# A mask moved from the first stage's products into the contraction's chunks, with two changes of order

## The chip, the cores and the metric

The kernel runs on one core of a Trainium2 chip. The core has five engines that work side by side: TensorE (PE, matmuls), VectorE (DVE), ScalarE (ACT), GpSimd (POOL) and SyncE (SP), which here only issues DMAs. They meet through semaphores. The metric is the device time of one execution in microseconds (us), as the median of several runs; less is better.

## The reference

The input x is 256 x 256 pixels of 64 channels, all in fp32. With m the mask (256 x 256), what is computed is:

```
a      = layernorm(channel_norm(x))                     # over the 64 channels
left   = m * (a @ WL + bL) * sigmoid(a @ GL + gL)
right  = m * (a @ WR + bR) * sigmoid(a @ GR + gR)
t[i,j,c] = sum_k left[i,k,c] * right[j,k,c]             # one 256x256x256 product for each channel
x1     = x + (layernorm(t) @ WO + bO) * sigmoid(a @ G + g)
out    = x1 + mixture(layernorm(x1))                    # 8 experts 64x64, the best 2 by a router
```

The change concerns the factor m of left and right.

## The kernel before

There are three stages, and each engine runs its own program, written out by hand, with waits on semaphores.

**First stage.** x comes in 8 super-blocks of 32 rows, a row being 128 partitions x 2 pixels (q = 0, 1) x 64 channels. For each super-block VectorE makes the statistics (`bn`, L860), GpSimd the scale and shift (`rstd_a`, L356 to L365) and the normalized rows (`norm_a`: a multiplication L380, an addition L384, eight rows each). TensorE turns four rows at a time (`turn`, L646) and multiplies each pair of rows by the four weights (`project`, L658) into `pr_a`, a ring of three pairs in PSUM: the first half holds left and right, the second the gates. ScalarE puts the sigmoid of the gates into `sig_a` (L510). VectorE then does in `left_right` (L873), for each row of a pair and each q, one product `pr_a * mask * sig_a` of 128 columns: four for a pair, 512 in all. The mask enters as a scalar for each partition, `mt[:, row, q]`. The products go into `stage` (two blocks of 16 rows) and from there to `left_right_scratch` in DRAM (`block_a`). VectorE's own order puts the statistics of super-block s + 2 between the products of super-block s, from the seventh pair on. The SP queue issues, in its order: loads of x (each waits until GpSimd has scaled the super-block that held the buffer), stores of blocks, and toward the end early loads of the first chunks.

**Contraction.** The 64 channels are done in 8 chunks of 8 channels. `chunk` has two buffers of four parts, left and right for q = 0 and 1, 2048 columns each. `load_blocks` fetches a chunk, the left parts when an earlier packing has freed them, the right parts when TensorE has finished the chunk before the last. All parts of a buffer count on one semaphore, `chunk_in[b]`. GpSimd's `pack_left` (L401) copies the left parts into another order (two instructions of 2048 columns a chunk; in chunk 0 the last two blocks, which come straight from `stage` by `direct`, have two small ones of their own) and waits for the whole chunk. The packing of a chunk may begin when TensorE is done with the chunk before the last. TensorE (`chunk_b`, L696) makes for each of the 8 channels k two halves of 256 rows in one of four banks of `ein`; ScalarE copies the even k to `t_all` (L533), VectorE the odd k (L922), in a loop over the chunks. TensorE waits for the copy of k before it writes k + 4.

**Last stage.** 64 units of 8 columns by 128 partitions, in slots: slot u handles the experts of unit u, the gate of unit u + 4 and the output of unit u - 1. Each engine goes through its list in `slot`. A unit has eight tiles m = 0 to 7. TensorE broadcasts the routing weight (`bcast`, L783), for tiles 0, 2, 4, 6 and, in even units, 7 VectorE multiplies it by the doubled input (`scale`, L1036); for tiles 1, 3, 5 and in odd units 7 ScalarE copies it out first (L579) and GpSimd multiplies (L451). `expert(ep)` (L796) takes the tiles 2 ep and 2 ep + 1. ScalarE's `double` (L563) copies the input of the next unit to both halves of the partitions, its `gate` (L553) makes the sigmoid for which TensorE's `x_turn` (L727) waits, and `y_turn` (L804) turns the result of the unit before.

Of the kernel before, what the change touches and what calls it, by code (L numbers as in the profile page):

```python
# [8 lines left out]
ALU = mybir.AluOpType  # L9
# [95 lines left out]
def metaformer_kernel(nc, x, mask, weights, router_w, router_b, expert_w, expert_b, out):  # L105
# [6 lines left out]
    with ExitStack() as ctx:  # L112
# [3 lines left out]
        def keep(name, shape, dt=F32):  # L116
            return ctx.enter_context(nc.sbuf_tensor(name, shape, dt))
# [29 lines left out]

        setup_bytes = 4 * (12 * C + 4 + 6 * C + 6 * C + P + E * C + E + 2 * P + 2 * N)
        (xts, _, w_proj, mt, r_all, b_all, xa, xs, sig_a, stage, bst, nv, nh, ny, nt) = layer([
            ("xts", [P, 2, TURN * P]), ("skip_setup", [P, setup_bytes // 4 - 2 * TURN * P + 16]),  # L150
            ("w_proj", [P, 6 * C]),
            ("mt", [P, N, Q]), ("r_all", [P, N, Q]), ("b_all", [P, N, Q]),
            ("xa", [P, 2, SUPER, Q * C]), ("xs", [P, 2, SUPER, Q * C]),
# [16 lines left out]
        def left_packed(c, b):  # L170
# [5 lines left out]

        (_, sel, kind, xc, xn, tn, ttn, xtn, sig_c, x2t, x2d, zb, bcs, wt, outc, bst_t, bst_x, y32, rr, bt, lg, ls, m1, m2, pm, ws, pk) = layer([
            ("t_keep", [P, C, 2 * N]),
            ("sel", [P, 2, E, C], F32R), ("kind", [P, 4, E]),
            ("xc", [P, XC, UNIT_J, C]), ("xn", [P, UNIT_J, C]), ("tn", [P, UNIT_J, C]),  # L180
            ("ttn", [P, WIDE]), ("xtn", [P, WIDE]), ("sig_c", [P, WIDE]), ("x2t", [P, X2, WIDE]), ("x2d", [P, 2, 2, WIDE]),
            ("zb", [P, NZ, WIDE]), ("bcs", [P, 2, WIDE]), ("wt", [P, 2, WIDE], F32R),
            ("outc", [P, 2, UNIT_J, C]), ("bst_t", [P, 2, TOK // 2, 6]), ("bst_x", [P, 2, TOK // 2, 6]),
            ("y32", [P, 2 * TOK]), ("rr", [P, 2, 2 * TOK]), ("bt", [P, 2, TOK]), ("lg", [P, 2, TOK, E]), ("ls", [P, TOK, E]),
            ("m1", [P, TOK]), ("m2", [P, TOK]), ("pm", [P, TOK]), ("ws", [P, 2, TOK]),
            ("pk", [P, TOK, 2, 2 * E], F32R)])

# [50 lines left out]
        def _(sp):  # L239
# [10 lines left out]
            def load_blocks(c, b, blocks, parts=range(2 * Q)):  # L250
                for u in parts:
                    part = lr_dram.rearrange("n p (u c) -> u p n c", u=2 * Q)[u, :, blocks, c * RUN:(c + 1) * RUN]
                    sp.dma_start(chunk[:, b, u, blocks, :], part).then_inc(chunk_in[b], 16)

# [71 lines left out]
        def _(pool):  # L326
# [69 lines left out]

            loads = 2 * Q * 16

            def pack_left(c, b, blocks):
                for q in range(Q):  # L400
                    ins = pool.tensor_copy(  # L401
                        left_packed(c, b)[:, q, :, :].rearrange("p c (n r) -> p n c r", r=ROWS)[:, blocks, :, :],
                        chunk[:, b, 2 * q, blocks, :].rearrange("p n (c r) -> p n c r", c=CHUNK))
                return ins

            pool.wait_ge(xs_ready, SUPERS * PIECES)
            pool.wait_ge(chunk_in[0], PARTS[0] * loads)
            pack_left(0, 0, slice(0, BLOCKS - 2))
            pool.wait_ge(direct_in, loads)
            pack_left(0, 0, slice(BLOCKS - 2, BLOCKS)).then_inc(packed, 1)  # L410
            for c in range(1, CHUNKS):
                pool.wait_ge(chunk_in[c % 2], (c // 2 + PARTS[c % 2]) * loads)
# [74 lines left out]
        def _(act):  # L487
# [6 lines left out]
            for h in range(2):  # L494
                for q in range(Q):
                    ins = act.activation(mt[:, h * P:h * P + P, q], ps_set[:, 1, (2 * h + q) * P:(2 * h + q + 1) * P], ACT.Copy)
            ins.then_inc(set_act, 1)
# [92 lines left out]
            def slot(u, ku):  # L590
                odd = ku % 2 == 1
                if has(u):
                    bcast(3, u, ku)
                if has(u + 4):
                    front(u + 4)
                if odd and has(u + 1):
                    soft((u - 1) // 2)
                if has(u):
                    bcast(5, u, ku)
                if has(u + 1):  # L600
                    double(u + 1, ku + 1, 0)
# [18 lines left out]
        def _(pe):  # L620
# [194 lines left out]
            def slot(u, ku):  # L815
# [36 lines left out]
        def _(dve):  # L852
# [11 lines left out]
            def left_right(p):  # L864
# [324 lines left out]
```

## Time and profile before

| what | value |
|---|---|
| median of 3 runs | 1099.11 us (1098.92 to 1100.91) |
| the profiled execution's own time | 1097.87 us |
| its span in the profile | 1096.1 us |
| busy: PE, DVE, ACT, POOL | 1005.4, 869.5, 639.3, 749.7 us |
| first stage, to VectorE's last product | 215.2 us |
| contraction, to TensorE's last matmul | 335.0 us |
| data moved by DMA | 119.38 MB |

The profile is of one execution; its span begins with the first instruction and ends with the last. The busy times are averages over stages with different limits, so a change is read in its own stage: which engine the others wait for there.

### The profile page before, as it was taken

The page shows a single profiled execution, that of the slowest core. Times are in us where ns is not written, and L with a number is a line of the kernel's source. Part 1 is how long each engine was busy: PE and PEld are TensorE (multiplying, and loading weights), DVE is VectorE, ACT ScalarE, POOL GpSimd, SP SyncE. Part 2 cuts the span into 40 slices and gives each one's busy share as a digit, 9 for nine tenths or more (in the row PEclk, how much of TensorE's full clock was granted, in tenths as well). Part 3 has the DMA queues.
Part 4 walks back from the last instruction along what each step waited for, and adds up shares of the span by engine and source line. Part 5 has one row for each costly group of instructions (what it writes and reads, how often), then busy time and mean ns, then how long its engine had stood idle before and what let it go on. Part 6 is the DMA issues. An engine that isn't in the chain of part 4 may idle for free.

```text
span 1096.1 us, 18926 instructions
## 1 busy us (share of the span) xinstructions
PE 1005.4 (92%) x5658; PEld 552.8 (50%) x5658; DVE 869.5 (79%) x3030; ACT 639.3 (58%) x1134; POOL 749.7 (68%) x727
## 2 busy tenths in 40 slices
PE   4889999899994599999999999999999999999996
PEld 2566666688883344444444444444444444444432
DVE  5899999812216678898889988998899889988884
ACT  2556666611111356767676767676767767676754
POOL 5998888212223367878787878787878877787844
PEclk9999999999996689999999999999999999999999
DMA  7688679989951001111111111111111111111001
GB/s 181 193 281 296 231 259 299 344 272 294 293 158 39 20 25 53 39 58 39 60 39 59 40 59 39 58 40 59 40 55 42 49 50 44 54 40 59 30 30 39
DMA packets 98904, 119.38 MB, mean 109 GB/s; under 512 B 6390, under 2 KB 72182, under 8 KB 96758
## 3 DMA queue, kind: packets, MB, share of 16 engines
q1 hardware_dynamic: 97670, 117.75, 33.7%
q8 instruction: 46, 0.75, 0.3%
q10 hardware_dynamic: 1136, 0.46, 0.2%
q14 instruction: 52, 0.43, 0.1%
HBM read 67.33 MB, written 50.33 MB: 107 GB/s over the span
## 4 chain that ended last, share of the span: by engine, by line
PE 60%; ACT 16%; DVE 12%; issue 4%; DMA 4%; POOL 3%; SPq 0%; DVEq 0%; ACTq 0%; POOLq 0%
PE b_m L796 15%; PE ein L696 8%; PE ring L783 7%; PE b_d L744 7%; ACT x2d L563 6%; DVE stage L873 6%; PE pr_a L658 4%; PE b_g L727 4%; PE b_g L721 3%; ACT ttn L546 3%; DVE bst L860 3%; PE b_g L734 3%; PE b_t L721 3%; DMA chunk<-left_right_scratch 2%; ACT sig_c L553 2%
## 5 line engine op out<-in xcount | busy, mean ns | idle before, releaser
L451 POOL TENSOR_TENSOR zb<-bcs,x2d 128x512 f32<-128x512 f32 x224 | 286.4, 1281 | 170.5 <-ACT bcs L579 170.4
L796 PE MATMUL b_m<-zb,w_exp 128*64 128x512 f32 x1024 | 275.5, 617 | 0.2
L1036 DVE TENSOR_TENSOR zb<-ring,x2d 128x512 f32<-128x512 f32 x288 | 197.7, 687 | 61.4 <-PE ring L783 57.0
L579 ACT ACTIVATE bcs<-ring 128x512 f32<-128x512 f32 x224 | 133.3, 595 | 160.0 <-PE ring L783 155.8
L563 ACT ACTIVATE x2d<-x2t 64x512 f32<-64x512 f32 x256 | 160.6, 628 | 3.4
L873 DVE SCALAR_TENSOR_TENSOR stage<-pr_a,mt,sig_a 128x128 f32<-128x128 f32 x512 | 147.8, 419 | 11.3 <-ACT sig_a L510 11.2
L658 PE MATMUL pr_a<-w_proj,xts 64*128 64x256 f32 x1024 | 138.3, 400 | 14.5 <-DVE stage L873 14.0
L783 PEld LDWEIGHTS ring<-wt,sel 64*128 64x128 f32 x512 | 47.9, 184 | 168.4 <-DVE zb L1036 81.2
L783 PE MATMUL ring<-wt,sel 64*128 64x512 f32 x512 | 127.6, 495 | 3.1 <-DVE zb L1036 2.3
L510 ACT ACTIVATE sig_a<-pr_a 128x512 f32<-128x512 f32 x128 | 76.5, 597 | 71.3 <-PE pr_a L658 71.2
L658 PEld LDWEIGHTS pr_a<-w_proj,xts 64*128 64x128 f32 x1024 | 95.3, 190 | 42.9 <-issue 23.6
L437 POOL TENSOR_TENSOR tn<-t_all,rr 128x512 f32<-128x512 f32 x64 | 86.8, 1357 | 35.5 <-DVE rr L964 21.0
L922 DVE COPY t_all<-ein 128x512 f32 x32 | 22.1, 691 | 93.2 <-PE ein L696 93.2
L744 PE MATMUL b_d<-turn_route,x2t 128*128 128x144 f32 x512 | 84.0, 310 | 3.3 <-DVE x2t L1053 3.3
L696 PE MATMUL ein<-chunk,t_all 128*128 128x256 f32 x384 | 83.6, 380 | 1.2 <-POOL t_all L401 1.2
L796 PEld LDWEIGHTS b_m<-zb,w_exp 128*64 128x64 f32 x1024 | 51.0, 134 | 62.4 <-issue 60.2
L744 PEld LDWEIGHTS b_d<-turn_route,x2t 128*128 128x128 f32 x512 | 69.7, 198 | 19.4 <-issue 14.6
L696 PEld LDWEIGHTS ein<-chunk,t_all 128*128 128x128 f32 x384 | 72.8, 190 | 11.8 <-issue 1.9
L734 PE MATMUL b_g<-xtn,w_og 64*64 64x512 f32 x256 | 71.1, 629 | 7.6 <-ACT ttn L546 7.6
L546 ACT ACTIVATE ttn<-b_t 64x512 f32<-64x512 f32 x128 | 75.8, 592 | 1.5
L533 ACT ACTIVATE t_all<-ein 128x512 f32 x32 | 19.1, 597 | 96.9 <-PE ein L696 96.9
L1059 DVE BATCH_NORM_STATS2 bst_x<-b_d 128x6 f32<-128x128 f32 x256 | 67.2, 285 | 5.9 <-PE b_d L744 5.9
(131 smaller groups left out, 1784.7 us busy)
## 6 DMA issues: line engine op xcount, KB each, us to landing
left_right_scratch<-stage SPq DMA_DIRECT2D x16, 2048.0 KB, 7.9
chunk<-left_right_scratch SPq DMA_DIRECT2D x24, 1024.0 KB, 9.1
xc<-in_x SPq DMA_DIRECT2D x64, 256.0 KB, 2.8
out<-outc SPq DMA_DIRECT2D x64, 256.0 KB, 2.0
chunk<-left_right_scratch SPq DMA_DIRECT2D x12, 384.0 KB, 7.8
chunk<-left_right_scratch SPq DMA_DIRECT2D x8, 192.0 KB, 5.1
chunk<-left_right_scratch SPq DMA_DIRECT2D x4, 256.0 KB, 8.0
chunk<-left_right_scratch SPq DMA_DIRECT2D x8, 64.0 KB, 4.8
```

Source lines behind the costliest of these rows:

```text
L451: pool.tensor_tensor(zb[:, m % NZ, :], bcs[:, tiles_before(POOL_TILES, ku, ku, m) % 2, :], x2d[:, ku % 2, m % 2, :], ALU.mult)\
L546: ins = act.activation(ttn[half * C:(half + 1) * C, :], b_t[(1 - half) * C:(2 - half) * C, :], ACT.Copy)
L563: ins = act.activation(x2d[half * C:(half + 1) * C, kw % 2, t, :], x2t[t * C:(t + 1) * C, kw % X2, :], ACT.Copy)
L579: act.activation(bcs[:, tiles_before(POOL_TILES, ku, ku, m) % 2, :], ring[:, bcast_bank(ku % 2, m), :], ACT.Copy).then_inc(bcast_out, 1)
L658: ins = pe.matmul(pr_a[:, k, q, r * LRG:(r + 1) * LRG], xts[half, g % 2, col:col + P], w_proj[half, 0:LRG], start=True, stop=True)
L696: m = pe.matmul(ein[:, k % 4, h * N:h * N + N], left_packed(c, b)[:, q, k, h * P:h * P + P], right[:, q, :, k, :], start=q == 0, stop=q == 1)
L734: g = pe.matmul(b_g[half[t], :], w_og[half[t], 0, :], xtn[half[t], :], start=True, stop=True)
L744: m = pe.matmul(b_d[:, j // 2, j % 2 * BACK:(j % 2 + 1) * BACK], x2t[:, kw % X2, pairs[j]], turn_route[:, :], start=True, stop=True)
L783: pe.matmul(ring[:, bcast_bank(ku % 2, m), :], sel[rows, ku % 2, m // 2 * 2:m // 2 * 2 + 2, :].rearrange("p e c -> p (e c)"), wt[rows, ku ...
L796: ins = pe.matmul(b_m[t * C:(t + 1) * C, :], w_exp[:, ep, :], zb[:, (2 * ep + t) % NZ, :], start=False, stop=ep == EP - 1, skip_group_chec ...
L873: ins = dve.scalar_tensor_tensor(stage[:, n % 2, q, :, row], pr_a[:, p % PAIR_RING, q, r * LRG:r * LRG + 2 * C], mt[:, n * ROWS + row:n * ...
L1036: dve.tensor_tensor(zb[:, m % NZ, :], ring[:, bcast_bank(ku % 2, m), :], x2d[:, ku % 2, m % 2, :], ALU.mult)\
```

## The change

It has three parts.

1. *Mask.* `left_right` is now one product of `pr_a` and `sig_a` of 512 columns for a pair, without the mask. GpSimd's packing multiplies the left part by the mask instead of copying it. VectorE multiplies the right parts by the mask in place (`mask_right`, two instructions of 2048 columns a chunk, four in chunk 0), and TensorE waits for it on the new semaphore `masked`. The mask of chunks 0 and 1 is done before VectorE's loop over the chunks, that of chunk c + 1 after the copy k = 5 of chunk c. `mt` lies in another order, and `ttn` takes its memory over later. VectorE's loop over the chunks is written out.
2. *Counts.* The parts of a chunk count on two semaphores: left parts on `left_in[b]`, for which GpSimd waits, right ones on `chunk_in[b]`, for which VectorE and TensorE wait.
3. *Order in the last stage.* ScalarE does `gate(u + 4)` before the second `double`, TensorE does `expert(2)` before `y_turn`.

```
 def load_blocks(c, b, blocks, parts=range(2 * Q)):
-    sp.dma_start(chunk[:, b, u, blocks, :], part).then_inc(chunk_in[b], 16)
+    sp.dma_start(chunk[:, b, u, blocks, :], part).then_inc(chunk_in[b] if u % 2 else left_in[b], 16)
...
+def mask_of(q, blocks):
+    return mt[:, q, :].rearrange("p (n r) -> p n r", r=ROWS)[:, blocks, :].unsqueeze(2)\
+        .broadcast_to([P, blocks.stop - blocks.start, CHUNK, ROWS])
...
 def pack_left(c, b, blocks):                      # GpSimd
-    ins = pool.tensor_copy(
+    ins = pool.tensor_tensor(
         left_packed(c, b)[:, q, :, :].rearrange("p c (n r) -> p n c r", r=ROWS)[:, blocks, :, :],
-        chunk[:, b, 2 * q, blocks, :].rearrange("p n (c r) -> p n c r", c=CHUNK))
+        chunk[:, b, 2 * q, blocks, :].rearrange("p n (c r) -> p n c r", c=CHUNK), mask_of(q, blocks), ALU.mult)
-pool.wait_ge(chunk_in[0], PARTS[0] * loads)
+pool.wait_ge(left_in[0], PARTS[0] * loads)
...
 # ScalarE's slot
+    if has(u + 4):
+        gate(u + 4)
     if has(u + 1):
         double(u + 1, ku + 1, 1)
-    if has(u + 4):
-        gate(u + 4)
...
 # TensorE
     pe.wait_ge(packed, c + 1)
+    pe.wait_ge(masked, c + 1)
...
     if has(u + 4):
         out_gate(u + 4)
+    if has(u):
+        expert(2, u, ku)
     if has(u - 1):
         y_turn(u - 1, ku - 1)
-    if has(u):
-        expert(2, u, ku)
...
 # VectorE, left_right
-    for r in range(PAIR):
-        row = p * PAIR % ROWS + r
-        for q in range(Q):
-            ins = dve.scalar_tensor_tensor(
-                stage[:, n % 2, q, :, row], pr_a[:, p % PAIR_RING, q, r * LRG:r * LRG + 2 * C],
-                mt[:, n * ROWS + row:n * ROWS + row + 1, q], sig_a[:, p % PAIR_RING, q, r, :], ALU.mult, ALU.mult)
-    ins.then_inc(lr_done, 1)
+    row, k = p * PAIR % ROWS, p % PAIR_RING
+    dve.tensor_tensor(stage[:, n % 2, :, :, row:row + PAIR].rearrange("p q c r -> p q r c"),
+                      pr_a[:, k, :, :].rearrange("p q (r c) -> p q r c", r=PAIR)[:, :, :, 0:2 * C],
+                      sig_a[:, k, :, :, :], ALU.mult).then_inc(lr_done, 1)
...
-with dve.Fori(0, CHUNKS) as c:
+def mask_right(b, blocks):
+    for q in range(Q):
+        right = chunk[:, b, 2 * q + 1, blocks, :].rearrange("p n (c r) -> p n c r", c=CHUNK)
+        ins = dve.tensor_tensor(right, right, mask_of(q, blocks), ALU.mult)
+    return ins
+
+def chunk_landed(c):
+    dve.wait_ge(chunk_in[c % 2], (c // 2 + PARTS[c % 2]) * Q * 16)
+
+chunk_landed(0)
+mask_right(0, slice(0, BLOCKS - 2))
+dve.wait_ge(direct_in, 2 * Q * 16)
+mask_right(0, slice(BLOCKS - 2, BLOCKS)).then_inc(masked, 1)
+chunk_landed(1)
+mask_right(1, slice(0, BLOCKS)).then_inc(masked, 1)
+for c in range(CHUNKS):
     for k in range(1, CHUNK, 2):
         dve.wait_ge(ein_ready, c * CHUNK + k + 1)
-        dve.tensor_copy(t_all[:, bass.ds(c * CHUNK + k, 1), :].rearrange("p a n -> p (a n)"), ein[:, k % 4, :])\
-           .then_inc(ein_dve, 1)
+        dve.tensor_copy(t_all[:, c * CHUNK + k, :], ein[:, k % 4, :]).then_inc(ein_dve, 1)
+        if k == 5 and 0 < c < CHUNKS - 1:
+            chunk_landed(c + 1)
+            mask_right((c + 1) % 2, slice(0, BLOCKS)).then_inc(masked, 1)
```

## Rows read from the trace of the kernel before

**Rows 1.** Window: length; busy PE, PEld, DVE, ACT, POOL; clock, DMA share, GB/s.
```profile
120.00:160.00 40.00, 35.82 (x268) 25.04 (x266) 38.59 (x158) 23.71 (x40) 31.64 (x46) 1.00 0.76 264
```

**Rows 2.** Timeline of GpSimd in the first stage: start, us, engine, line, tiles, idle.
```profile
80.19 0.27 POOL L356 TENSOR_SCALAR nv<-bst 128x64 f32<-128x64 f32 x1
...
86.47 3.76 POOL L380 TENSOR_TENSOR xs<-xa,r_all 128x1024 f32<-128x1024 f32 x2
...
90.19 3.76 POOL L384 TENSOR_TENSOR xs<-xs,b_all 128x1024 f32<-128x1024 f32 x2
...
104.05 0.27 POOL L356 TENSOR_SCALAR nv<-bst 128x64 f32<-128x64 f32 x1 [2.66 <-DVE bst L860]
...
176.04 0.28 POOL L356 TENSOR_SCALAR nv<-bst 128x64 f32<-128x64 f32 x1 [2.77 <-DVE bst L860]
```

**Rows 3.** Timeline of all engines, the first stage's last turns and products.
```profile
205.93 0.65 PE L646 MATMUL xt_a<-turn_route,xs 128*128 128x128 f32 x4
...
208.44 0.66 PE L646 MATMUL xt_a<-turn_route,xs 128*128 128x128 f32 x4
...
210.84 4.37 DVE L873 SCALAR_TENSOR_TENSOR stage<-pr_a,mt,sig_a 128x128 f32<-128x128 f32 x16 [0.26 <-ACT sig_a L510]
```

**Rows 4.** Costliest groups of the page: busy us, mean ns, idle before.
```profile
L451 POOL TENSOR_TENSOR zb<-bcs,x2d 128x512 f32<-128x512 f32 x224 | 286.4, 1281 | 170.5 <-ACT bcs L579 170.4
...
L1036 DVE TENSOR_TENSOR zb<-ring,x2d 128x512 f32<-128x512 f32 x288 | 197.7, 687 | 61.4 <-PE ring L783 57.0
...
L873 DVE SCALAR_TENSOR_TENSOR stage<-pr_a,mt,sig_a 128x128 f32<-128x128 f32 x512 | 147.8, 419 | 11.3 <-ACT sig_a L510 11.2
```

**Rows 5.** Timeline of all engines, from the first stage into the contraction.
```profile
216.52 4.24 POOL L401 COPY xa<-chunk 128x1792 f32<-128x1792 f32 x4 [19.27 <-DMA chunk<-left_right_scratch]
...
220.00 0.50 DVE L916 TENSOR_TENSOR bias_lo<-eb_wide,bias_hi 128x256 fp32r<-128x256 f32 x1
...
220.90 15.74 PE L696 MATMUL ein<-chunk,xa 128*128 128x256 f32 x64 [3.18 <-POOL xa L401]
...
229.43 3.73 POOL L401 COPY t_all<-chunk 128x2048 f32<-128x2048 f32 x2 [8.68 <-DMA chunk<-left_right_scratch]
...
236.47 13.98 PE L696 MATMUL ein<-chunk,t_all 128*128 128x256 f32 x64
```

**Rows 6.** The chain that ended last, the load of chunk 2's right half.
```profile
237.07 10.05 DMA chunk<-left_right_scratch
```

**Rows 7.** Timeline of all engines in chunk 2: its start, the copy k = 5.
```profile
251.04 4.15 PE L696 MATMUL ein<-chunk,t_all 128*128 128x256 f32 x18 [0.59 <-POOL t_all L401]
...
261.82 0.69 DVE L922 COPY t_all<-ein 128x512 f32 x1 [2.76 <-PE ein L696]
```

**Rows 8.** Timeline: VectorE and GpSimd products from SBUF at one time.
```profile
346.55 0.69 DVE L1071 TENSOR_TENSOR xn<-xc,rx 128x512 f32<-128x512 f32 x1 [1.67 <-PE b_t L721]
...
346.61 1.81 POOL L437 TENSOR_TENSOR tn<-t_all,rr 128x512 f32<-128x512 f32 x1 [2.40 <-PE b_t L721]
...
347.27 1.70 DVE L1073 TENSOR_TENSOR xn<-xn,bx 128x512 f32<-128x512 f32 x1
```

**Rows 9.** One microsecond of chunk 0, columns as in rows 1.
```profile
222.00:223.00 1.00, 1.00 (x3) 0.75 (x3) 0.00 (x0) 0.00 (x0) 0.00 (x0) 0.50 1.24 524
```

**Rows 10.** Timeline of the last stage: GpSimd's tile 5, TensorE's y turn.
```profile
506.33 1.28 POOL L451 TENSOR_TENSOR zb<-bcs,x2d 128x512 f32<-128x512 f32 x1
...
507.36 0.66 PE L804 MATMUL ring<-turn_route,x2t 128*128 128x128 f32 x4
```

**Rows 11.** The chain that ended last, through an odd and an even unit.
```profile
599.70 1.18 PE b_d L744 x8
...
609.39 0.44 PE ring L811 x4
...
611.27 1.18 PE b_d L744 x8
...
621.87 1.18 PE b_d L744 x8
```

More of the change, by code:

```diff
@@ L130, in metaformer_kernel @@
         bx = keep("bx", [P, 2 * N])
+        mt = keep("mt", [P, Q, N])
         def layer(tensors, psums=()):
@@ L148, in metaformer_kernel @@
         setup_bytes = 4 * (12 * C + 4 + 6 * C + 6 * C + P + E * C + E + 2 * P + 2 * N)
-        (xts, _, w_proj, mt, r_all, b_all, xa, xs, sig_a, stage, bst, nv, nh, ny, nt) = layer([
+        (xts, _, w_proj, r_all, b_all, xa, xs, sig_a, stage, bst, nv, nh, ny, nt) = layer([
             ("xts", [P, 2, TURN * P]), ("skip_setup", [P, setup_bytes // 4 - 2 * TURN * P + 16]),
             ("w_proj", [P, 6 * C]),
-            ("mt", [P, N, Q]), ("r_all", [P, N, Q]), ("b_all", [P, N, Q]),
+            ("r_all", [P, N, Q]), ("b_all", [P, N, Q]),
             ("xa", [P, 2, SUPER, Q * C]), ("xs", [P, 2, SUPER, Q * C]),
@@ L174, in left_packed @@
             return left_odd if b else left_even
-        (_, sel, kind, xc, xn, tn, ttn, xtn, sig_c, x2t, x2d, zb, bcs, wt, outc, bst_t, bst_x, y32, rr, bt, lg, ls, m1, m2, pm, ws, pk) = layer([
+        def mask_of(q, blocks):
+            return mt[:, q, :].rearrange("p (n r) -> p n r", r=ROWS)[:, blocks, :].unsqueeze(2)\
+                .broadcast_to([P, blocks.stop - blocks.start, CHUNK, ROWS])
+        (_, sel, kind, xc, xn, tn, xtn, sig_c, x2t, x2d, zb, bcs, wt, outc, bst_t, bst_x, y32, rr, bt, lg, ls, m1, m2, pm, ws, pk) = layer([
             ("t_keep", [P, C, 2 * N]),
@@ L180, in metaformer_kernel @@
             ("xc", [P, XC, UNIT_J, C]), ("xn", [P, UNIT_J, C]), ("tn", [P, UNIT_J, C]),
-            ("ttn", [P, WIDE]), ("xtn", [P, WIDE]), ("sig_c", [P, WIDE]), ("x2t", [P, X2, WIDE]), ("x2d", [P, 2, 2, WIDE]),
+            ("xtn", [P, WIDE]), ("sig_c", [P, WIDE]), ("x2t", [P, X2, WIDE]), ("x2d", [P, 2, 2, WIDE]),
             ("zb", [P, NZ, WIDE]), ("bcs", [P, 2, WIDE]), ("wt", [P, 2, WIDE], F32R),
@@ L186, in metaformer_kernel @@
             ("pk", [P, TOK, 2, 2 * E], F32R)])
+        ttn = mt[:, :, :].rearrange("p q n -> p (q n)")
         (b_t, b_g, b_d, b_r, b_m, ring) = layer([], [
@@ L211, in metaformer_kernel @@
         turn_ready = sem("turn_ready"); turned = sem("turned")
-        chunk_in = [sem("chunk_in0"), sem("chunk_in1")]
-        direct_in = sem("direct_in"); packed = sem("packed"); ein_ready = sem("ein_ready"); ein_act = sem("ein_act"); ein_dve = sem("ein_dve")
+        chunk_in = [sem("right_in0"), sem("right_in1")]; left_in = [sem("left_in0"), sem("left_in1")]
+        direct_in = sem("direct_in"); packed = sem("packed"); masked = sem("masked"); ein_ready = sem("ein_ready"); ein_act = sem("ein_act"); ein_dve = sem("ein_dve")
         xc_in = [sem("xc_in0"), sem("xc_in1"), sem("xc_in2")]; sel_made = sem("sel_made")
@@ L395, in _ @@
                 norm_a(s, (2, 3))
-            loads = 2 * Q * 16
+            loads = Q * 16
             def pack_left(c, b, blocks):
                 for q in range(Q):
-                    ins = pool.tensor_copy(
+                    ins = pool.tensor_tensor(
                         left_packed(c, b)[:, q, :, :].rearrange("p c (n r) -> p n c r", r=ROWS)[:, blocks, :, :],
-                        chunk[:, b, 2 * q, blocks, :].rearrange("p n (c r) -> p n c r", c=CHUNK))
+                        chunk[:, b, 2 * q, blocks, :].rearrange("p n (c r) -> p n c r", c=CHUNK), mask_of(q, blocks), ALU.mult)
                 return ins
             pool.wait_ge(xs_ready, SUPERS * PIECES)
-            pool.wait_ge(chunk_in[0], PARTS[0] * loads)
+            pool.wait_ge(left_in[0], PARTS[0] * loads)
             pack_left(0, 0, slice(0, BLOCKS - 2))
-            pool.wait_ge(direct_in, loads)
+            pool.wait_ge(direct_in, 2 * loads)
             pack_left(0, 0, slice(BLOCKS - 2, BLOCKS)).then_inc(packed, 1)
             for c in range(1, CHUNKS):
-                pool.wait_ge(chunk_in[c % 2], (c // 2 + PARTS[c % 2]) * loads)
+                pool.wait_ge(left_in[c % 2], (c // 2 + PARTS[c % 2]) * loads)
                 if c > 1:
@@ L495, in _ @@
                 for q in range(Q):
-                    ins = act.activation(mt[:, h * P:h * P + P, q], ps_set[:, 1, (2 * h + q) * P:(2 * h + q + 1) * P], ACT.Copy)
+                    ins = act.activation(mt[:, q, h * P:h * P + P], ps_set[:, 1, (2 * h + q) * P:(2 * h + q + 1) * P], ACT.Copy)
             ins.then_inc(set_act, 1)
@@ L683, in chunk_b @@
             def chunk_b(c, b):
-                loads = 2 * Q * 16
+                loads = Q * 16
                 first = PARTS[b] * loads
@@ L687, in chunk_b @@
                 if isinstance(c, int) and c == 0:
-                    pe.wait_ge(direct_in, loads)
+                    pe.wait_ge(direct_in, 2 * loads)
                 pe.wait_ge(packed, c + 1)
+                pe.wait_ge(masked, c + 1)
                 right = chunk[:, b, :, :, :].rearrange("p (q s) n (c r) -> p q s n c r", s=2, c=CHUNK)[:, :, 1, :, :, :]
```

## The prediction

> **What bounds the kernel now.** I read the windows first, then the chain that ended last, then the timelines of the places where the chain changes its engine.
>
> The first stage (to 215.2 us) is VectorE's. In 120 to 160 us it is busy 38.6 of 40 us, TensorE 35.8, GpSimd 31.6 [rows 1]. GpSimd starts a new super-block (32 rows) 24 us after the last one, and waits 2.66 us of that for VectorE's statistics: 104.05 in [rows 2] carries the wait, 80.19 none. Its own work is therefore 104.05 - 2.66 - 80.19 = 21.2 us a super-block. TensorE needs 2.51 us for each four rows when nobody holds it [rows 3], 20.1 us for 32. So VectorE (24.0) is first, GpSimd (21.2) and TensorE (20.1) close behind.
>
> The contraction (eight chunks) is TensorE's: a chunk takes 13.98 us, and the next begins 14.57 us after it began where a transfer and a packing lie between [rows 5, 7]. It is tight: right halves land 10.05 us after they are asked for [rows 6]. Here VectorE and GpSimd have much idle time, but both are in TensorE's loop.
>
> The last stage is 32 pairs of units. The even unit takes 621.87 - 611.27 = 10.60 us, the odd one 11.57 [rows 11]. TensorE's work in the odd one is only one turn of 0.44 us more, so it stalls 11.57 - 10.60 - 0.44 = 0.53 us, behind ScalarE, whose sigmoid comes after four copies.
>
> **First stage: what goes.** 512 three-operand products of 128 columns become 128 products of 512. The busy time gives 147.8/512 = 0.289 us each, 1.15 us a pair; the nearest row for the new one (PSUM times SBUF, 512 columns, same engine) is 0.687 [rows 4]. It saves 0.46 us a pair, 7.4 a super-block: VectorE falls from 24.0 to about 17 us. The output's stride is the old one and was paid in the old products, so I add nothing. The bound is not 17 but GpSimd's 21.2. From 80.19 four more of its super-blocks in a row put the start of the last at 80.19 + 4 x 21.2 = 165.0 instead of 176.04. The first eight rows are ready 90.19 - 80.19 + 1.9 = 11.9 us later [rows 2], at 176.9; seven more turns of 2.51 give 194.5; and from the last turn to VectorE's last product 215.21 - 208.44 = 6.8 us [rows 3], less some 0.5 since the last four products no longer queue, give 200.8. Gain: 215.2 - 200.8 = **-14.4 us**, not the 6 x 7 that VectorE alone would give. The SP queue holds block stores behind the loads of x, which wait for GpSimd's scaling; that comes at GpSimd's pace as well, so I allow 0 to 2 us of loss for it.
>
> **Contraction: where the mask goes.** GpSimd's packing turns from a copy into a product with two inputs. For the product of 2048 the bounds are 2 x 1.88 = 3.8 us (1024 columns with one broadcast input, 3.76 for two) and 4 x 1.281 = 5.1 (512 columns, both inputs full) [rows 2, 4]. The mask's inner run is full, so I take 4.5, that is 9.0 for a chunk. It starts when the chunk before begins, since the left half is now counted alone, and ends by +9 to +10 of a 14 us chunk: hidden, unless it is late. VectorE gets two products of 2048 columns. From 0.69 us for 512 [rows 8], one column a cycle, they are 2.3 each (0.69 x 4 = 2.8 above): **4.6 us a chunk, on the path**.
>
> *Chunks 2 to 7.* The mask of the next chunk stands in VectorE's queue behind the copy k = 5. After a wait that copy begins 261.82 - 251.04 = 10.78 us into the chunk and ends at 11.47 [rows 7]; the right half has landed by 10.1 [rows 6]. The mask runs from 11.5 to 16.1, and TensorE begins 0.1 later. So each chunk takes 16.2 us instead of 14.0 (twice 14.57), with the copy k = 7 queued behind the mask too, which delays nobody else. Six such steps: 6 x 16.2 - (2 x 14.57 + 4 x 13.98) = 97.2 - 85.1 = **+12.1 us**. The earlier packing saves only the two waits of 0.6 that this sum already drops.
>
> *Chunks 0 and 1.* Count from VectorE's last product (215.2). Before, TensorE began chunk 0 at +5.7 and chunk 1 at +21.3. GpSimd's packing of chunk 0 starts at +1.3 and would take 2 x 4.0 + 2 x 0.7 us (1792 and 256 columns at the same price) instead of the 4.24 of the copies; VectorE is free at +5.3 [rows 5]. Then the two meet. In [rows 8] VectorE's product runs 0.69 us undisturbed, and 1.70 when it starts while GpSimd's product of 1.81 us is under way: it ended 0.55 us after GpSimd's did, as if it had waited for the end and then run. The mask products have two SBUF inputs like that one. I let them run one after the other: packing to +9.3, then masks and the small last pieces alternately, masked at about +15, TensorE starts chunk 0 there. Chunk 1's data are there at +14.2 (229.43 [rows 5]), and VectorE waits for them and masks them before it copies the first odd column of chunk 0. With the packing of chunk 1 between, that lasts to +26; TensorE has done five of eight columns and waits. Three columns later, at +26.0 + 0.7 + 5.3 = +32, chunk 1 begins: **+10.7 us**. Bounds: +30 (GpSimd at 3.8, VectorE first) and +41 (next part).
>
> *The clock.* The idle 3.18 us before 220.90 were followed by a granted clock of 0.50, the 1.2 GHz level [rows 5, 9], and chunk 0 took 15.74 instead of 13.98: 1.8 us. The new gaps are 2.0 us each, for which I have no row. 0 to 6 x 1.8 = 10.8; I take **+3**.
>
> **Last stage.** ScalarE's sigmoid before the second pair of copies comes 1.27 us earlier, and would take away the 0.53 us of each odd unit: 32 x 0.53 = 17 us. But TensorE now does expert(2) before the y turn, and expert(2) needs GpSimd's tile 5, which ends at 506.33 + 1.28 = 507.61 where TensorE is free at 507.36 [rows 10]: 0.25 us of wait in every unit, even and odd alike. The odd one then ends 0.29 earlier, the even one 0.25 later. I take **0**, and 0.1 us of error in either reading is 6 us.
>
> **Sum.** 1096.1 - 14.4 + 12.1 + 10.7 + 3 + 0 = 1107.5 us of span. The profiled execution took 1.8 us more than its span (1097.87), and the median of the runs is 1.2 above it: 1107.5 + 3.0 = **1110.5 us**, +1.0%.
>
> **Rivals.**
> 1. *Strict turns at the start.* If after every instruction the other engine goes first, the two small masks of chunk 0 (the last two blocks) each wait for one 4.5 us packing of chunk 1. Chunk 0 is masked at +25 instead of +15, VectorE then masks chunk 1 at once, nothing stalls again, and chunk 1 begins at 25 + 14 + 1.8 = +41: 9 us more, about 1120. For it: one pair of rows with the waiting. Against: it needs chunk 1's left half to have landed before +15, which is close. 
> 2. *The last stage gains (the other side).* Should TensorE not wait for tile 5 (POOL spans are rough), 17 us go: 1094, faster. It decides from 11.4 + 2.2 = 13.6 of the 17 us on, that is, if the wait is under 0.05 us a unit. For it: expert(2) never waits for GpSimd now. Against: it stands 0.6 us later now.
> 3. *The clock falls in every chunk*: +7.8 on the sum, 1118.
> 4. *The masks cost nothing*, since right halves land earlier than k = 5 allows and VectorE overlaps: 1110.5 - 12.1 = 1098. The order of its queue speaks against it.
>
> **From cases to numbers.** My forecast 0.5 (own range 1104 to 1117), strict turns 0.2, clock 0.1, last-stage gain 0.12, masks free 0.03, the rest 0.05. The bounds of the prices add 5 either way; the range that leaves out 2 in 10 is 1097 to 1122. A measurement of this kernel tells about 0.2% (2.2 us) from no change. Faster 0.13 (rival 2, part of 4), same 0.05, slower 0.82.
>
> **What would show each step.** Right: products of 0.69 us in the first stage, GpSimd without waits for statistics after 80 us, last product near 201; a mask after each k = 5 and chunk starts 16.2 us apart; TensorE waiting for VectorE's mask before chunks 2 to 7 and for a copy in chunk 0; expert(2) waiting for GpSimd's tile 5. Wrong: chunk starts at 14 us, a first stage that ends later than 205, or units whose sum is off 22.17 us by over 0.2.

## The result, and the profile after

The changed kernel takes 1120.86 us (median of 4 runs, 1120.26 to 1123.33); before took 1099.01 on the same chip (4 runs, 1097.98 to 1100.91). The ratio is 1.020 (95% interval 1.0183 to 1.0217): slower by 2.0% (between 1.8 and 2.2), where 1.0% was predicted (1110.5). The profiled execution took 1120.89 us with a span of 1119.1, 23.0 more than before's 1096.1.

Two groups of part 5 of the page of the profile after (columns as in [rows 4]):

```profile
L806 PE MATMUL b_m<-zb,w_exp 128*64 128x512 f32 x1024 | 276.2, 616 | 21.0 <-POOL zb L460 19.4
...
L881 DVE TENSOR_TENSOR stage<-pr_a,sig_a 128x512 f32<-128x512 f32 x128 | 127.1, 1034 | 22.0 <-ACT sig_a L519 20.4
```

L881 is the new product of the first stage: 1034 ns each, not 687. L806 is `expert`: it sat idle for 21.0 us, 19.4 of them for GpSimd's tile. I read the rest in the order of the prediction's sum.

**First stage.** The timeline of VectorE before the change, the products of two pairs (four instructions each), with three statistics between them:

```profile
136.84 1.20 DVE L873 SCALAR_TENSOR_TENSOR stage<-pr_a,mt,sig_a 128x128 f32<-128x128 f32 x4
...
138.47 1.19 DVE L873 SCALAR_TENSOR_TENSOR stage<-pr_a,mt,sig_a 128x128 f32<-128x128 f32 x4
```

And after it, a pair's product among the statistics, and the last product:

```profile
134.58 1.03 DVE L881 TENSOR_TENSOR stage<-pr_a,sig_a 128x512 f32<-128x512 f32 x1
...
136.03 1.03 DVE L881 TENSOR_TENSOR stage<-pr_a,sig_a 128x512 f32<-128x512 f32 x1
...
204.93 1.01 DVE L881 TENSOR_TENSOR stage<-pr_a,sig_a 128x512 f32<-128x512 f32 x1 [0.22 <-ACT sig_a L519]
```

And of GpSimd, the first instruction of two super-blocks:

```profile
145.28 0.27 POOL L365 TENSOR_SCALAR nv<-bst 128x64 f32<-128x64 f32 x1 [0.86 <-DVE bst L870]
...
167.34 0.27 POOL L365 TENSOR_SCALAR nv<-bst 128x64 f32<-128x64 f32 x1 [0.88 <-DVE bst L870]
```

VectorE starts a product, and with three statistics behind it the next product, every 136.03 - 134.58 = 1.45 us; before the same turn took 138.47 - 136.84 = 1.63. GpSimd's period is 22.06 us (145.28 to 167.34), 0.88 of it a wait for the statistics; before it was 24.0 with 2.7 [rows 2]. The last product ends at 204.93 + 1.01 = 205.94 instead of 215.21: **-9.3 us**. This term carries about 1 us of scatter: in the six profiles with the old first stage (`before` and five kernels below) the last product ends between 215.16 and 217.20, in the six with the new one (`after` and five below) between 205.71 and 206.77.

**From the first stage to chunk 1.** Timelines of single stretches around the masks of chunk 0 (a row shows only the instructions that its window touches):

```profile
207.28 11.28 POOL L410 TENSOR_TENSOR xa<-chunk,mt 128x1792 f32<-128x1792 f32 x4 [18.74 <-DMA chunk<-left_right_scratch]
...
211.45 4.06 DVE L923 TENSOR_TENSOR bias_lo<-eb_wide,bias_hi 128x256 fp32r<-128x256 f32 x1
...
215.44 2.54 DVE L929 TENSOR_TENSOR chunk<-chunk,mt 128x1792 f32<-128x1792 f32 x1
...
216.06 2.50 POOL L410 TENSOR_TENSOR xa<-chunk,mt 128x256 f32<-128x256 f32 x1
...
217.90 2.54 DVE L929 TENSOR_TENSOR chunk<-chunk,mt 128x1792 f32<-128x1792 f32 x1
...
219.81 4.98 POOL L410 TENSOR_TENSOR t_all<-chunk,mt 128x2048 f32<-128x2048 f32 x1 [1.25 <-DMA chunk<-left_right_scratch]
...
220.36 4.71 DVE L929 TENSOR_TENSOR chunk<-chunk,mt 128x256 f32<-128x256 f32 x1
...
224.75 4.67 POOL L410 TENSOR_TENSOR t_all<-chunk,mt 128x2048 f32<-128x2048 f32 x1
...
225.00 4.71 DVE L929 TENSOR_TENSOR chunk<-chunk,mt 128x256 f32<-128x256 f32 x1
...
229.85 16.05 PE L706 MATMUL ein<-chunk,xa 128*128 128x256 f32 x64 [19.89 <-DVE chunk L929]
```

GpSimd's two long packings (1792 columns) run from 207.28 to 215.2. `bias_lo` (L923, an instruction with two SBUF inputs that took 0.50 us in [rows 5]) starts at 211.45 and ends at 215.51, 0.3 us after them. From there the engines alternate, one instruction each: behind the first small packing (256 columns) VectorE's mask of 1792 columns, the second small packing, the second mask of 1792. Then comes GpSimd's packing of chunk 1, 4.98 us, and VectorE's mask of 256 columns, started 0.55 us after it, needs 4.71; the second mask of 256 columns needs 4.71 as well, behind the second packing. In the chain that ended last the four masks of chunk 0 are one piece:

```profile
215.51 14.21 DVE chunk L929 x4
```

TensorE starts chunk 0 at 229.85, that is +23.9 from the last product (before: +5.7). Chunk 1 starts at 245.74, +39.8 instead of +21.3: **+18.5 us**.

**Chunks 1 to 7.** The chain that ended last, from chunk 1 into chunk 2:

```profile
256.30 0.69 DVE t_all L944
...
256.99 4.41 DVE chunk L929 x2
```

The timeline of TensorE, the contraction's chunks (L706 is `chunk_b`):

```profile
245.74 13.98 PE L706 MATMUL ein<-chunk,t_all 128*128 128x256 f32 x64
...
261.63 14.08 PE L706 MATMUL ein<-chunk,t_all 128*128 128x256 f32 x64 [1.92 <-DVE chunk L929]
...
277.65 15.76 PE L706 MATMUL ein<-chunk,t_all 128*128 128x256 f32 x64 [1.94 <-DVE chunk L929]
...
346.68 3.69 PE L706 MATMUL ein<-chunk 128*128 128x256 f32 x16 [1.93 <-DVE chunk L929]
```

Each of the chunks 2 to 7 waits 1.9 us for the mask, which stands behind the copy k = 5 (L944), as drawn. But in some chunks the same 64 matmuls take 15.76 instead of 14.08. Three windows, columns as in [rows 1]:

```profile
262.00:264.00 2.00, 2.00 (x11) 1.77 (x10) 0.00 (x0) 0.24 (x1) 1.78 (x1) 1.00 1.02 292
...
278.00:280.00 2.00, 2.00 (x7) 1.62 (x6) 0.00 (x0) 0.00 (x0) 2.00 (x1) 0.57 1.09 309
...
282.00:284.00 2.00, 2.00 (x11) 1.74 (x11) 0.69 (x1) 0.00 (x0) 2.00 (x1) 1.00 1.15 345
```

The granted clock is 1.00 (2.4 GHz) at the start of the chunk that began at 261.63, and 0.57 (nearly the 1.2 GHz level) at the start of the one at 277.65, where it is back at 1.00 from 282 us on. Both chunks followed an idle gap of 1.92 to 1.94 us. Chunk 1 to chunk 7 takes 346.68 - 245.74 = 100.94 us where before took 84.57: **+16.4**.

**Last stage.** The chain that ended last, through one odd and one even unit (as [rows 11]):

```profile
602.25 1.18 PE b_d L754 x8
...
608.12 1.29 POOL zb L460
...
609.54 1.08 PE b_m L806 x4
...
613.52 1.18 PE b_d L754 x8
...
624.36 1.18 PE b_d L754 x8
```

The timeline of TensorE at the first of these waits:

```profile
609.54 1.08 PE L806 MATMUL b_m<-zb,w_exp 128*64 128x512 f32 x4 [0.31 <-POOL zb L460]
```

The odd unit takes 11.27 us, the even one 10.84; before 11.57 and 10.60 [rows 11]. From the start of chunk 7 to the end of the span it is 772.42 us instead of 775.06: **-2.6**. Together -9.3 + 18.5 + 16.4 - 2.6 = +23.0.

### The profile page after: what moved, and what is told of

The parts are those of the page before. It is cut to its first block, busy times and chain, and to the rows that moved or that the text cites. A ratio compares the mean times of both kernels' runs of the same rounds, so it can differ in the third digit from the quotient of the medians.

```text
span 1119.1 us, 18486 instructions
## 1 busy us (share of the span) xinstructions
PE 1004.0 (90%) x5658; PEld 559.2 (50%) x5658; DVE 895.9 (80%) x2664; ACT 644.4 (58%) x1134; POOL 799.0 (71%) x727
## 4 chain that ended last, share of the span: by engine, by line
PE 48%; POOL 21%; DVE 14%; issue 11%; ACT 4%; DMA 2%; DVEq 0%; POOLq 0%; SPq 0%
PE b_m L806 13%; PE ein L706 9%; POOL zb L460 9%; PE b_d L754 7%; POOL tn L446 6%; PE ring L793 5%; DVE stage L881 4%; PE pr_a L667 4%; DVE chunk L929 4%; PE ring L814 3%; ACT bcs L588 3%; POOL xn L445 3%; DVE bst L870 3%; PE b_g L737 2%; DMA left_right_scratch<-stage 2%
## 5 line engine op out<-in xcount | busy, mean ns | idle before, releaser
L806 PE MATMUL b_m<-zb,w_exp 128*64 128x512 f32 x1024 | 276.2, 616 | 21.0 <-POOL zb L460 19.4
L881 DVE TENSOR_TENSOR stage<-pr_a,sig_a 128x512 f32<-128x512 f32 x128 | 127.1, 1034 | 22.0 <-ACT sig_a L519 20.4
L806 PEld LDWEIGHTS b_m<-zb,w_exp 128*64 128x64 f32 x1024 | 52.5, 135 | 123.0 <-DVE zb L1060 69.2
L706 PE MATMUL ein<-chunk,t_all 128*128 128x256 f32 x384 | 89.4, 396 | 9.6 <-DVE chunk L929 9.6
L410 POOL TENSOR_TENSOR t_all<-chunk,mt 128x2048 f32<-128x2048 f32 x12 | 59.0, 4938 | 42.4 <-PE ein L706 34.1
L706 PEld LDWEIGHTS ein<-chunk,t_all 128*128 128x128 f32 x384 | 76.1, 199 | 22.8 <-issue 11.6
L944 DVE COPY t_all<-ein 128x512 f32<-128x512 f32 x32 | 22.1, 690 | 79.4 <-PE ein L706 79.4
L555 ACT ACTIVATE mt<-b_t 64x512 f32<-64x512 f32 x128 | 75.7, 591 | 1.5
```

Of the source, the lines that this page charges most:

```text
L706: m = pe.matmul(ein[:, k % 4, h * N:h * N + N], left_packed(c, b)[:, q, k, h * P:h * P + P], right[:, q, :, k, :], start=q == 0, stop=q == 1)
L806: ins = pe.matmul(b_m[t * C:(t + 1) * C, :], w_exp[:, ep, :], zb[:, (2 * ep + t) % NZ, :], start=False, stop=ep == EP - 1, skip_group_chec ...
L881: dve.tensor_tensor(stage[:, n % 2, :, :, row:row + PAIR].rearrange("p q c r -> p q r c"), pr_a[:, k, :, :].rearrange("p q (r c) -> p q r ...
```

## The experiments

The kernels are named by what they do; numbers are medians, with the ratio to before on the same chip and its interval.

### The two orders of the last stage, and the counts

Four kernels take one or two parts of the change into the kernel before. `gate_only`:

```
# ScalarE's slot, kernel before
+    if has(u + 4):
+        gate(u + 4)
     if has(u + 1):
         double(u + 1, ku + 1, 1)
-    if has(u + 4):
-        gate(u + 4)
```

> The kernel before with one edit: ScalarE's gate(u + 4) ahead of the second double. My theory: the 0.53 us stall of each odd unit goes and, since expert(2) stays behind the y turn, nothing waits for GpSimd's tile 5: pairs of units 22.17 - 0.53 = 21.64 us, 32 x 0.53 = 17 us less, about 1082. Rival: the second double is late for the next unit (it now waits behind the gate, which waits for TensorE's out_gate) and holds VectorE's and GpSimd's tiles: 1095 to 1100.

Measured: 1089.26 us, ratio 0.9906 (0.9886 to 0.9926), before 1099.59: 10.3 us faster. The odd unit takes 11.23 us, the even one still 10.60. The forecast was 1082: of the stall of 0.53 us only 11.57 - 11.23 = 0.34 went, and 0.19 stayed. Where it stayed shows in the timeline of VectorE and TensorE at the y turn of an odd unit:

```profile
604.07 0.68 DVE L1036 TENSOR_TENSOR zb<-ring,x2d 128x512 f32<-128x512 f32 x1
...
604.10 0.59 PE L734 MATMUL b_g<-xtn,w_og 64*64 64x512 f32 x1
...
604.80 0.42 PEld L804 LDWEIGHTS ring<-turn_route,x2t 128*128 128x128 f32 x4 [1.00 <-DVE zb L1036]
...
604.81 0.65 PE L804 MATMUL ring<-turn_route,x2t 128*128 128x128 f32 x4
```

The y turn (L804) starts when VectorE's tile is done, 0.71 us after the last matmul of the gate began (604.10 to 604.81); in the even unit that follows it starts 0.52 us after it (615.33 to 615.85). The difference is the 0.19. The 1.00 in brackets is idle time of the weight loads, while TensorE's matmuls still ran. The chain passes there through VectorE's routing arithmetic (L1008 to L1015), which stands before that tile in its queue. The gain of this order ended at the next engine in line, after 32 x 0.34 = 10.9 us by the units.

`expert_only` takes the other order:

```
# TensorE's slot, kernel before
+    if has(u):
+        expert(2, u, ku)
     if has(u - 1):
         y_turn(u - 1, ku - 1)
-    if has(u):
-        expert(2, u, ku)
```

> The kernel before with one edit: TensorE's expert(2) ahead of the y turn. My theory: expert(2) waits some 0.3 us for GpSimd's tile 5 in every unit; the even unit gets 0.25 us longer, the odd one stays at ScalarE's sigmoid: 32 x 0.25 = 8 us more, about 1107. Rival (the wait is hidden by TensorE's queue): 1099.

Measured: 1107.19 us, ratio 1.0063 (1.004 to 1.0085): 7.6 us slower. The turns b_d of successive units start at 560.78, 572.34 and 583.17, so the odd unit is as long as before (11.56) and the even one 10.84 instead of 10.60. 32 x 0.24 = 7.7 us: the wait for tile 5 that [rows 10] allowed to be read.

`both_orders` has the two edits:

> The kernel before with both changes of order and nothing else: the last stage of the changed kernel. Theory: its 22.11 us a pair of units, 1097. If the last stage gained more and the contraction lost more than I read from the traces: under 1094.

Measured over 10 runs: 1095.76 us, ratio 0.9969 (0.9957 to 0.9981): 3.8 us faster; the two alone add up to -2.7. Units of 10.84 and 11.27 us, as in the changed kernel.

`counts_only` takes the counts of left and right parts alone:

```
-    sp.dma_start(chunk[:, b, u, blocks, :], part).then_inc(chunk_in[b], 16)
+    sp.dma_start(chunk[:, b, u, blocks, :], part).then_inc(chunk_in[b] if u % 2 else left_in[b], 16)
...
-    pool.wait_ge(chunk_in[c % 2], ...)
+    pool.wait_ge(left_in[c % 2], ...)
```

> The kernel before with left and right halves counted apart, GpSimd still copying. Theory: the packing no longer waits for the right half, so the two waits of 0.6 us before chunks 2 and 4 go: chunks begin 14.0 us apart, 1098. Rival: the earlier packing lets the next left half be fetched earlier and delays right halves: 1099 to 1102.

Measured over 10 runs: 1097.33 us, ratio 0.9986 (0.9975 to 0.9998), 2.3 us faster. The timeline of TensorE, six chunks without a wait:

```profile
236.69 83.04 PE L696 MATMUL ein<-chunk,t_all 128*128 128x256 f32 x384
...
319.57 13.98 PE L696 MATMUL ein<-chunk 128*128 128x256 f32 x64
```

The two waits of 0.6 us [rows 7] are gone, and six steps take 82.9 us instead of 84.6. But the steps vary by themselves: `gate_only`, which has the old counts, takes 83.6 for them. So the counts give 0.7 to 1.7 us by the steps, and 2.3 by the medians.

### The product of the first stage

`wide_product` puts the new product of 512 columns into the kernel before. The mask is multiplied nowhere.

```
-    for r in range(PAIR):
-        ...
-            ins = dve.scalar_tensor_tensor(stage[:, n % 2, q, :, row], ..., ALU.mult, ALU.mult)
+    dve.tensor_tensor(stage[:, n % 2, :, :, row:row + PAIR].rearrange("p q c r -> p q r c"), ..., ALU.mult).then_inc(lr_done, 1)
```

> The kernel before with the one product of 512 columns a pair, and the mask multiplied in nowhere. It isolates the first stage. The changed kernel's trace shows 0.94 us a product instead of my 0.69, so VectorE stays first at 22.0 us a super-block: last product near 206, 9 us less, 1090, and chunk starts as before. If 0.69 had been right, GpSimd would bound it: 201, 1085.

`wide_plain` has the same product with its output written without gaps. The mask is multiplied nowhere here too, and left and right go to the scratch in another order than the contraction reads.

```
-    stage[:, n % 2, :, :, row:row + PAIR].rearrange("p q c r -> p q r c")
+    stage[:, n % 2].rearrange("p q c r -> p (q c r)")[:, row // PAIR * 512:row // PAIR * 512 + 512]
+        .rearrange("p (q r c) -> p q r c", q=Q, r=PAIR)
```

> As wide_product, but each product is written without gaps in stage instead of at every 16th element, so left and right lie in the wrong order in the scratch. Theory: the stride of the output costs the 0.25 us, a product takes 0.69 us, GpSimd becomes first (21.2 us a super-block), last product near 201, 1085. Rival: the order of the loops or PSUM costs it: 0.94 us again, 1090.

Measured: `wide_product` 1090.03 us, ratio 0.9915 (0.9893 to 0.9936); `wide_plain` 1084.67, ratio 0.9863 (0.984 to 0.9886); before 1099.50. In `wide_product` the product takes 1001 to 1076 ns and the last one ends at 206.7, GpSimd's period is 22.0 to 22.1 with 0.8 to 0.9 of waiting: the first stage of the changed kernel, without the rest of it. In `wide_plain` it takes 666 to 693 ns. Its timeline, VectorE's same turn of one product and three statistics, and the last product:

```profile
135.22 0.67 DVE L871 TENSOR_TENSOR stage<-pr_a,sig_a 128x512 f32<-128x512 f32 x1
...
136.40 0.68 DVE L871 TENSOR_TENSOR stage<-pr_a,sig_a 128x512 f32<-128x512 f32 x1
...
199.62 0.69 DVE L871 TENSOR_TENSOR stage<-pr_a,sig_a 128x512 f32<-128x512 f32 x1 [0.22 <-ACT sig_a L510]
```

And GpSimd's super-blocks in the same kernel:

```profile
122.50 0.28 POOL L356 TENSOR_SCALAR nv<-bst 128x64 f32<-128x64 f32 x1
...
143.77 0.27 POOL L356 TENSOR_SCALAR nv<-bst 128x64 f32<-128x64 f32 x1
```

1.18 us a turn, and GpSimd waits no more: 21.27 us a super-block, last product at 200.3. The prediction had 21.2 and 200.8 from 0.687 us. So the mechanism and the pace of GpSimd were right, and what was wrong is the product's price: its output goes to every 16th element of `stage` (64 bytes apart).

### The start of the contraction

`left_copy` is the changed kernel with GpSimd's packing a copy again. Left gets no mask.

```
-    ins = pool.tensor_tensor(left_packed(c, b)..., chunk[:, b, 2 * q, blocks, :]..., mask_of(q, blocks), ALU.mult)
+    ins = pool.tensor_copy(left_packed(c, b)..., chunk[:, b, 2 * q, blocks, :]...)
```

> The changed kernel with GpSimd copying the left halves again (they get no mask). Theory: the two engines still shut each other out at the start, but GpSimd's turns are 1.7 to 1.9 us instead of 4.0 to 4.6: masks of chunk 0 done at about +15 instead of +24 after the last product, chunk 1 begins at about +31 instead of +40; chunks 2 to 7 still 16.0 apart or 17.7 where the clock falls, since they wait for VectorE alone: about 1112. Rival (GpSimd's length matters for chunks 2 to 7 too): those come under 15 us apart and 1100.

One run: 1108.85 us, span 1107.1. Chunk 0 starts at +10.2 from the last product, chunk 1 at +28.0; +15 and +31 were expected, and 1112. VectorE is done with `bias_lo` at 211.3 here, since no long packing holds it, and masks chunk 0 in 5.02 us. Here the stall appears that the prediction drew for the changed kernel: TensorE does 40 of 64 matmuls, five columns, and waits for VectorE, which stands in the masks of chunk 1. The timeline of TensorE:

```profile
216.36 11.43 PE L706 MATMUL ein<-chunk,xa 128*128 128x256 f32 x40 [7.09 <-DVE chunk L929]
...
228.87 5.45 PE L706 MATMUL ein<-chunk,xa 128*128 128x256 f32 x24 [1.07 <-DVE t_all L944]
```

So GpSimd's arithmetic costs 39.8 - 28.0 = 11.8 us at the start and, with 12.0 us between the two spans, next to nothing later. That does not say whether its length or its place hurts.

`pack1_held` leaves the lengths and changes the place: in the changed kernel the packing of chunk 1 waits until chunk 0 is masked.

```
 for c in range(1, CHUNKS):
+    if c == 1:
+        pool.wait_ge(masked, 1)
     pool.wait_ge(left_in[c % 2], ...)
```

> The changed kernel with one wait more: GpSimd packs chunk 1 only when chunk 0 is masked. Theory (strict turns): the two small masks no longer wait behind packings of 4.6 us; chunk 0 begins at +16 instead of +24, masks of chunk 1 take turns with its packing until +30, TensorE stops after five columns and chunk 1 begins at about +33 to +35 instead of +40: 1114 to 1116. Rival (chunk 1's packing then is the last): no gain, 1121.

Measured: 1113.55 us, ratio 1.0132 (1.0108 to 1.0155), 7.3 us less than the changed kernel. The chain that ended last has the four masks of chunk 0 in

```profile
216.86 5.61 DVE chunk L931 x4
```

5.61 us instead of 14.21, and chunk 0 starts at +15.8, chunk 1 at +31.2. The prediction's own numbers for this place were +15 and +32. The first is met by its mechanism: the two small masks no longer stand behind long packings. The second is met partly by chance: VectorE masks chunk 1 until 231.2, +24.4, and the stall of TensorE that the prediction drew in chunk 0 does not come. Chunk 0 goes through without a wait, 15.4 us from start to start.

### The mask's place, and the clock

`mask_k3` is the changed kernel with the mask of the next chunk behind the copy k = 3.

```
-    if k == 5 and 0 < c < CHUNKS - 1:
+    if k == 3 and 0 < c < CHUNKS - 1:
```

> The changed kernel with the mask of the next chunk behind the copy k = 3 instead of k = 5. Theory: the place in VectorE's queue costs 1.3 us a chunk; now the mask starts when the right half lands (8.6 to 10.1 us into the chunk), ends at 13.2 to 14.6, chunks begin 14.2 to 14.7 us apart instead of 16.0, the gaps are under 1 us and the clock no longer falls: 6 x 1.3 + 3 x 1.7 = 13 us less, 1108. Rival (the copy k = 5 held behind the mask stops TensorE): chunks 16 us apart as now, 1121.

Measured: 1108.12 us, ratio 1.0081 (1.0056 to 1.0107), before 1098.27. The timelines of TensorE, then of GpSimd and VectorE at two of the masks:

```profile
261.77 14.08 PE L706 MATMUL ein<-chunk,t_all 128*128 128x256 f32 x64 [1.38 <-DVE chunk L929]
...
276.68 14.08 PE L706 MATMUL ein<-chunk,t_all 128*128 128x256 f32 x64 [0.84 <-DVE chunk L929]
...
291.37 14.08 PE L706 MATMUL ein<-chunk,t_all 128*128 128x256 f32 x64 [0.61 <-DVE chunk L929]
...
263.02 9.07 POOL L410 TENSOR_TENSOR t_all<-chunk,mt 128x2048 f32<-128x2048 f32 x2 [7.25 <-DMA chunk<-left_right_scratch]
...
269.59 6.86 DVE L929 TENSOR_TENSOR chunk<-chunk,mt 128x2048 f32<-128x2048 f32 x2
...
286.63 4.49 DVE L929 TENSOR_TENSOR chunk<-chunk,mt 128x2048 f32<-128x2048 f32 x2 [2.05 <-DMA chunk<-left_right_scratch]
```

The gaps shrink from 1.9 us to between 0.61 and 1.38, and after them no chunk is slow any more: each takes 13.9 to 14.1 us. They do not vanish. The right half lands late in the chunk, and a mask that meets a packing takes 6.86 us for two instructions instead of 4.49.

### The versions that could beat both

`gate_counts` is the kernel before with the gate's order and the counts, and nothing else of the change.

> The kernel before with the earlier gate and the separate counts, without the other order and with the mask where it was: the parts that gained alone. Theory: 10 + 2 us, 1087. Rival (they overlap): 1089.

Measured: 1087.44 us (1086.60 to 1088.38), ratio 0.990 (0.988 to 0.9919), before 1098.27. It is the fastest version that still computes everything.

`all_mended` is the changed kernel with the held packing of chunk 1, the mask behind k = 3, and `y_turn` before `expert(2)` again.

> The changed kernel with its mask moved as it is, but the y turn ahead of expert(2) again, the mask behind k = 3 and the packing of chunk 1 held until chunk 0 is masked. Theory, by addition from 1121: - 7 (held), - 13 (k = 3), - 6.5 (order): 1094. Moving the mask then still costs 7 us against gate_counts. Rival (held and k = 3 share their gain): 1098 or more.

Measured: 1090.60 us (1090.34 to 1091.06), ratio 0.9932 (0.9914 to 0.995), 3.4 us under what the addition gave. Faster than before, and 3.2 us slower than `gate_counts`, which leaves the mask where it was. TensorE's chunks:

```profile
221.21 15.80 PE L708 MATMUL ein<-chunk,xa 128*128 128x256 f32 x64 [12.57 <-DVE chunk L931]
...
236.84 13.98 PE L708 MATMUL ein<-chunk,t_all 128*128 128x256 f32 x64
...
266.57 27.89 PE L708 MATMUL ein<-chunk,t_all 128*128 128x256 f32 x128 [0.86 <-DVE chunk L931]
...
324.78 13.98 PE L708 MATMUL ein<-chunk 128*128 128x256 f32 x64
```

The last product ends at 205.7 here, 10.8 us before that of `gate_counts` (216.6); chunk 0 starts at 221.21 against 222.41. Nearly the whole gain of the first stage is spent there: packing and masks run one after the other (+15.5 from the last product instead of +5.8). The six steps then take 87.9 us against 82.9. Moving the mask costs 3 us even in its best version here. Not tried was a version whose product is written without gaps and whose contraction reads that order; `wide_plain` leaves out what such a version would have to pay for the reading.

## Why the prediction was right in direction and 10 us short

The forecast of a slower kernel came true; the size did not, 1110.5 against 1120.86. By span the forecast was 1107.5 and the result 1119.1, 11.6 more; the step from span to time was 1.8 us and not 3.0. By the terms of the sum:

| term | predicted | measured | off by |
|---|---|---|---|
| first stage, to the last product | -14.4 | -9.3 | +5.1 |
| from there to chunk 1 | +10.7 | +18.5 | +7.8 |
| chunk 1 to chunk 7, mask and clock | +12.1 + 3 | +16.4 | +1.3 |
| last stage | 0 | -2.6 | -2.6 |

**First stage: the right mechanism, a term mis-sized.** The step that failed is "The output's stride is the old one and was paid in the old products, so I add nothing". The nearest row had the same engine, the same columns and inputs from PSUM and SBUF, but wrote without gaps. So the old side of the difference, 1.15 us a pair, held whatever the stride costs, and the new side, 0.687, did not. `wide_plain` shows that with such an output the forecast is exact (200.3 for 200.8), and `wide_product` that with the kernel's own output the same instruction takes 1.03 us. By the turns of one product and three statistics, 1.63 us before, 1.45 after and 1.18 without gaps, the merged product saved 0.18 us a pair and not 0.46. Whether the old products paid the same per column is not shown: they also had more instructions to start. The Trainium skill (SBUF — State Buffer, "Door 1: The DMA port swizzle (why `[64,N]` ≈ `[32,N]`)") says that each access that crosses to a new 16-byte line pays a penalty. The difference of 1.03 and 0.69 us agrees in its direction; the Trainium skill gives no size there. With 1.45 us a turn VectorE has no wait from 131.10 to 145.1, and the statistics come late again, so the first stage did not become GpSimd's alone. The prediction had named this as a sign of being wrong: a first stage that ends later than 205.

**The start of the contraction: rival 1 instead of the forecast.** The forecast let the small pieces and the masks alternate and then VectorE go on; it gave chunk 0 at +15 and chunk 1 at +32. Rival 1 had both small masks wait for one packing each, +25 and +41. Measured: +23.9 and +39.8, with 4.71 us for each small mask, and with the packing of chunk 1 held back (`pack1_held`) it is +15.8 and +31.2. What decided was the condition that the rival named: the left half of chunk 1 was there in time (219.81, +13.9 from the last product). The prediction called that close and gave it 0.2. One of its two conditions, the waiting, was already in [rows 8], so 0.2 was low. The step that failed here is "then masks and the small last pieces alternately, masked at about +15": it left out that the packings of chunk 1 take a turn each before the two small masks, which put the end of the masks at 229.72, +23.8. The rival's total of 1120 was met partly by luck: the first stage missed by 5 us one way, the last by 2.6 the other. The Trainium skill (SBUF — State Buffer, "Who interferes with whom") says that who starts first keeps the other out for the whole instruction, and the 4.71 us of a 256-column mask agree. GpSimd's product of 2048 columns was taken at 4.5 and measured 4.52 to 4.58 where nothing holds it; the 4.50 that rival 1 quotes is stated for an addition of two tensors. VectorE was free not at +5.3 but at +9.6, since `bias_lo` waited for the packings; as the masks were to wait for the packings until +9.3 anyway, that cost nothing more.

**Chunks 2 to 7: right, the clock's share by a guess.** The steps were drawn at 16.2 us and take 16.0 at the full clock, bounded by copy k = 5 and mask; the mask of 2048 columns takes 2.28 us for 2.3. That part is 6 x 16.0 - 84.6 = +11.4 for +12.1. The clock is the rest: it fell in three of the six chunks 2 to 7 (3, 5 and 6), at 1.7 us each, +5.0 for the +3 taken out of 0 to 10.8. `mask_k3` confirms both: gaps shorter by 0.5 to 1.3 us and no slow chunk behind them, some 12 us less. Why a gap of 1.9 us costs the clock in one chunk and not in the next is open.

**Last stage: right in both halves, small in sum.** The prediction's "the odd one then ends 0.29 earlier, the even one 0.25 later" is what was measured (-0.30, +0.24), and GpSimd's tile 5 is what `expert(2)` waits for. But it drew one sum of two independent edits. Apart they are -10.3 and +7.6 us (`gate_only`, `expert_only`), and the forecast of what the gate alone removes, 17 us in rival 2, was too high, because VectorE's tile is late next, by 0.19 us of the 0.53. Rival 3 (a slow clock in every chunk) and rival 4 (free masks) are refuted by the chunk starts.

## What to carry to other kernels

Take the edits of a bundle apart before judging it: here two swaps of two lines were worth -10 and +8 us, and the bundle's name hid both. Where VectorE and GpSimd both have SBUF work queued, a short instruction can cost as much as the longest of the other engine, so count the instructions on both sides of a critical hand-over and hold back those that nobody waits for yet: one wait more on GpSimd gave 7.3 us here. When a duration is borrowed from a row, compare the output's stride as well as the columns.

## What the runs showed of the hardware

- VectorE's product of 512 fp32 columns took 1.00 to 1.08 us writing every 16th element and 0.67 to 0.69 us writing without gaps, with the same inputs (`wide_product`, `wide_plain`).
- VectorE and GpSimd with two-input SBUF work queued on both took strict turns, instruction by instruction (`after`, 215 to 230 us): twice a mask of 256 columns took 4.71 us, behind packings of 4.98 and 4.67.
- A gap of TensorE of 1.91 to 1.94 us was followed by a granted clock near the 1.2 GHz level at the start of the chunk (1.7 us lost) in three of six chunks, in the changed kernel and also in `left_copy` and `pack1_held`, and not in the same three; after the gaps of 0.61 to 1.38 us of `mask_k3` and `all_mended` none was.
